# A gated cross-attention and low-rank feed-forward kernel: two small factors padded to 16 rows, the second first, the context's casts on GpSimd, and the first tile's low part multiplied last

## What is computed

```python
x = x + tanh(g_xattn[0]) * xattn(layernorm(x), ctx_1024)
x = x + tanh(g_ffn[0]) * ffn(layernorm(x), W, b, lora_down, lora_up, down_aux, up_aux)

def xattn(h, v):                       # softmax over the context's 77 rows
    p = softmax(einsum('bsd,bvd->bsv', h, v), axis=-1)
    return einsum('bsv,bvd->bsd', p, v)

def ffn(h, W, b, lora_down, lora_up, down_aux, up_aux):
    low = up_aux @ (lora_up @ (lora_down @ down_aux))
    return einsum('bsi,oi->bso', h, W) + b + einsum('bsi,oi->bso', h, low)
```

## Time and profile before

| | |
|---|---|
| median of 3 runs | 305.19 us (305.17 to 305.98) |
| the profiled execution, its whole time | 305.47 us |
| its span | 303.4 us |
| TensorE busy | 295.6 us |
| VectorE, GpSimd, ScalarE busy | 230.0, 224.5, 183.7 us |
| moved by DMA | 56.39 MB, mean 186 GB/s |

### The profile page before, as it was taken

One profiled execution on the slowest core, in us unless ns is written; L12 is line 12 of the kernel. 1 busy time (PEld: TensorE's weight loads), 2 busy tenths in 40 slices (PEclk: granted clock), 3 DMA queues, 4 the chain that ended last, 5 costly groups with the idle time before them and its releaser, 6 DMA issues.

```text
span 303.4 us, 6504 instructions
## 1 busy us (share of the span) xinstructions
PE 295.6 (97%) x2072; PEld 282.9 (93%) x2072; DVE 230.0 (76%) x797; ACT 183.7 (61%) x540; POOL 224.5 (74%) x274
## 2 busy tenths in 40 slices
PE   7999999999999999999999999999999999999992
PEld 5799999999999999999999999999999999999992
DVE  2877788885887788788498778777877788778865
ACT  2765675573775666566476666556665675567652
POOL 3478777785687877777578877787778777887763
PEclk9999999999999999999999999999999999999998
DMA  7754765442786494455265577544445555444003
GB/s 209 307 174 174 242 208 210 152 166 103 247 251 222 161 260 176 166 208 210 95 191 183 208 259 283 203 156 165 169 160 193 210 208 208 165 159 161 38 36 138
DMA packets 16750, 56.39 MB, mean 186 GB/s; under 512 B 2118, under 2 KB 2134, under 8 KB 16717
## 3 DMA queue, kind: packets, MB, share of 16 engines
q1 hardware_dynamic: 16281, 55.19, 52.7%
q10 hardware_dynamic: 436, 0.80, 0.8%
HBM read 35.84 MB, written 16.78 MB: 173 GB/s over the span
## 4 chain that ended last, share of the span: by engine, by line
PE 97%; DVE 1%; ACT 0%; issue 0%; POOL 0%; POOLq 0%; ACTq 0%; DVEq 0%
PE y_ps L598 68%; PE a_ps L647 10%; PE y_ps L652 10%; PE y_ps L629 2%; PE c_ps L588 2%; PE y_ps L565 1%; PE a_ps L605 1%; PE a_ps L570 1%; PE y_ps L697 0%; PE y_ps L616 0%; PE y_ps L705 0%; PE y_ps L701 0%; PE c_ps L579 0%; DVE o_sb L831 0%; ACT squares L498 0%
## 5 line engine op out<-in xcount | busy, mean ns | idle before, releaser
L598 PE MATMUL y_ps<-wc,xT 128*128 128x256 f32 x1524 | 224.9, 302 | 0.0
L598 PEld LDWEIGHTS y_ps<-wc,xT 128*128 128x128 f32 x1524 | 211.2, 189 | 2.0
L393 POOL TENSOR_TENSOR x_bias<-x,bias_g 128x512 f32<-128x512 f32 x63 | 81.5, 1294 | 58.2 <-DVE x L793 58.2
L381 POOL TENSOR_TENSOR xT<-xt_raw,xT 128x512 fp32r<-128x512 f32 x64 | 83.4, 1302 | 0.1
L484 ACT ACTIVATE expd<-y_ps,neg_max,rs 128x77 f32<-128x77 f32 x64 | 26.8, 418 | 81.1 <-DVE neg_max L780 81.1
L404 POOL TENSOR_TENSOR rs<-stat_eps,half_neg 128x2 f32<-128x2 f32 (+1 forms) x67 | 46.2, 689 | 5.2
L831 DVE SCALAR_TENSOR_TENSOR o_sb<-y_ps,rs,x_bias 128x512 f32<-128x512 f32 x64 | 47.5, 743 | 0.6 <-POOL rs L404 0.6
L498 ACT ACTIVATE squares<-x,x_nmean 128x512 f32<-128x512 f32 x64 | 45.4, 710 | 1.7 <-DVE x_nmean L801 1.6
L652 PEld LDWEIGHTS y_ps<-stacks,pT 110*128 110x128 f32 (+1 forms) x256 | 39.6, 190 | 5.7
L769 DVE BATCH_NORM_STATS2 bn<-x_sb 128x6 f32<-128x512 f32 x64 | 43.8, 684 | 0.0
L793 DVE SCALAR_TENSOR_TENSOR x<-a_ps,x_sb 128x512 f32<-128x512 f32 x64 | 43.4, 678 | 0.2 <-PE a_ps L647 0.2
(11 more groups left out here) (81 smaller groups left out, 192.6 us busy)
## 6 DMA issues: line engine op xcount, KB each, us to landing
x_sb<-in_x SPq DMA_DIRECT2D x32, 512.0 KB, 4.4
xt_raw<-in_xt SPq DMA_DIRECT2D x31, 512.0 KB, 5.2
out<-o_sb SPq DMA_DIRECT2D x31, 512.0 KB, 3.0
stacks<-v_hi SPq DMA_DIRECT2D x2, 308.0 KB
w_all<-in_w SPq DMA_DIRECT2D x2, 256.0 KB, 6.5
out<-o_sb SPq DMA_DIRECT2D x2, 256.0 KB, 2.0
stacks<-v_hi SPq DMA_DIRECT2D x2, 252.0 KB
stacks<-v_lo SPq DMA_DIRECT2D x2, 252.0 KB
```

The source lines that it names most:

```text
L381: pool.tensor_tensor(xT[:, k % TRING, 1, :, :], xt_raw[:, k % XRING // UNIT, k % UNIT, :, :], xT[:, k % TRING, 0, :, :].bitcast(F32), ALU. ...
L393: pool.tensor_tensor(x1_bias[:, q, :], x1[:, j, :], bias_g[:, :], ALU.add).then_inc(x1b_ready, 1)
L598: mm = pe.matmul(y_half(k, h)[:, 0:n], xT[:, k % TRING, part, c, :], wc[:, c, w, h * H:h * H + n], start=(c == 0 and part == 0 and w == 0) ...
```

## The change

- The host pads `low_in` from 100 to 112 rows and `low_out` from 50 to 64, with zeros (`whole_lanes`); more rows are loaded, but the padding of `low_in_sb` and `low_out_sb` adds only zeros to the products.
- On ScalarE's DMA queue low_out goes first, and the context's 77 rows follow as two DMAs, 64 and 13 rows; they stood first, as one.
- TensorE has five fillers instead of eight. The product for the second factor (up) comes first, and that of the first factor (down) after it in halves of 256 columns, the second half in another PSUM bank; ScalarE's and VectorE's copies are halved likewise (`down_hi`, `down_lo`), and the low-rank products wait for the half they need.
- VectorE finishes up_st ahead of centring the context.
- GpSimd, not ScalarE, makes v_hi of the first batch, and it, not ScalarE and VectorE, copies the columns `ct` into `wc`, around the cast of the first x.
- ScalarE takes the tanh of the gates before ct, not after it.
- VectorE makes v_lo ahead of W's low parts, not after them.
- In `first_scores` the products with W's high parts come first, then x's high part with the low parts, and x's low part last, with its own wait.

```diff
@@ -408,8 +412,16 @@
             def prep(n, k):
                 pass
+            pool.wait_ge(ld_ctx, 32)
+            pool.wait_ge(row0_ok, 1)
+            pool.wait_ge(tg_ok, 1)
+            pool.tensor_scalar(v_hi[0:VP, 0:D], c_rows[0:VP, :], tg[0:VP, 0:1], None, ALU.mult).then_inc(v_hi_ok, 1)
+            pool.wait_ge(ct_hi_ok, 1)
+            pool.tensor_copy(wc[:, :, 0, D:D + V], ct_part(0, 0)[:, :, 1:VP].bitcast(F32)).then_inc(c_cols, 1)
             xt_landed(pool, 0, 0)
             pool.tensor_copy(xT[:, 0, 0, :, :], xt_raw[:, 0, 0, :, :]).then_inc(x0_hi, 1)
+            pool.wait_ge(ct_lo_ok, 1)
+            pool.tensor_copy(wc[:, :, 1, D:D + V], ct_part(0, 1)[:, :, 1:VP].bitcast(F32)).then_inc(c_cols, 1)
             for k in (-2, -1):
                 step(k, k)
             pool.wait_ge(ld_b, 16)
@@ -418,19 +430,17 @@
         @block.scalar
         def _(act):
-            act.dma_start(c_rows[1:VP, :], ctx_in[0]).then_inc(ld_ctx, 16)
             act.dma_start(low_out_sb[:, :], low_out).then_inc(ld_out, 16)
+            cut = V // BY * BY
+            for a, z in ((0, cut), (cut, V)):
+                act.dma_start(c_rows[1 + a:1 + z, :], ctx_in[0, a:z, :]).then_inc(ld_ctx, 16)
             load_w(act, 1)
             act.dma_start(xt_raw[:, 0, 0, :, :].rearrange("p c r -> p (c r)"), xt_in[0, :, 0:D]).then_inc(ld_first_xt, 16)
             def ctx_rows_hi(n):
-                act.wait_ge(ld_ctx, 32 * n + 16)
-                if n == 0:
-                    act.wait_ge(row0_ok, 1)
-                    act.wait_ge(tg_ok, 1)
-                else:
-                    act.wait_ge(stacked[(n - 1) % 2], stack_landed(n - 1))
+                act.wait_ge(ld_ctx, 32 * n + 32)
+                act.wait_ge(stacked[(n - 1) % 2], stack_landed(n - 1))
                 if n == 2:
                     act.wait_ge(stacked[0], 16 * (FIRST + 3))
                 act.activation(v_hi[0:PACK[n], 0:D], c_rows[0:PACK[n], :], ACT.Copy, scale=tg[0:PACK[n], 0:1]).then_inc(v_hi_ok, 1)
@@ -537,22 +547,24 @@
                 if packs(t, TAKE):
                     ctx_product_hi(t // TB + 1)
+            def down_hi(h):
+                act.wait_ge(low_mm, 2 + h)
+                act.activation(dn_st[:, h * H:(h + 1) * H], down_bank(h), ACT.Copy).then_inc(dn_hi_ok, 1)
             act.wait_ge(low_mm, 1)
-            act.activation(dn_st[:, :], a_ps[0:LR, :], ACT.Copy).then_inc(dn_hi_ok, 1)
-            act.wait_ge(low_mm, 2)
             act.activation(up_st[:, :], up_bank(), ACT.Copy).then_inc(up_hi_ok, 1)
-            prep(0, TURN)
-            act.wait_ge(ct_hi_ok, 1)
-            act.activation(wc[:, :, 0, D:D + V], ct_part(0, 0)[:, :, 1:VP].bitcast(F32), ACT.Copy).then_inc(c_cols, 1)
+            down_hi(0)
+            down_hi(1)
             act.wait_ge(ld_w[0], 16)
             act.activation(tg[:, :], w_all[:, 0:2], ACT.Tanh).then_inc(tg_ok, 1)
             act.wait_ge(tg_ok, 1)
             act.activation(tg_row[:, :], tg[:, 0:1], ACT.Copy).then_inc(row_gate, 1)
+            prep(0, TURN)
             for c in range(KC):
                 act.wait_ge(w_tr, c + 1)
                 act.activation(wc[:, c, 0, 0:D], w_bank(c), ACT.Copy, scale=tg[:, 1:2]).then_inc(w_hi_ok, 1)
-            ctx_rows_hi(0)
             x_hi(1, 1)
             all_tiles(step, prep)
@@ -565,10 +577,19 @@
                     pe.matmul(y_ps[:, 0, 1, 0:P], ident[:, :], ident[:, :], start=True, stop=True)
             pe.wait_ge(ident_ok, 4)
-            stay_busy(8)
-            pe.wait_ge(ld_in, 16)
-            pe.matmul(a_ps[0:LR, :], low_in_sb[:, 0:LR], low_in_sb[:, LR:LR + D], start=True, stop=True)\
-                .then_inc(low_mm, 1)
+            stay_busy(5)
+            def low_up():
+                pe.wait_ge(ld_out, 16)
+                pe.matmul(up_bank(), low_out_sb[:, 0:LR], low_out_sb[:, LR:LR + D], start=True, stop=True).then_inc(low_mm, 1)
+            def low_down(h):
+                pe.wait_ge(ld_in, 16)
+                pe.matmul(down_bank(h), low_in_sb[:, 0:LR], low_in_sb[:, LR + h * H:LR + (h + 1) * H], start=True, stop=True)\
+                    .then_inc(low_mm, 1)
             def prep(n, k):
                 if k == TURN:
@@ -605,20 +626,27 @@
                 return pe.matmul(cw_ps(0), ct_part(0, lhs)[:, c, :], wc[:, c, rhs, 0:D], start=(c == 0 and lhs == 0 and rhs == 0),
                                  stop=(c == KC - 1 and rhs == 1), skip_group_check=True)
+            def score_part(c, part, w):
+                return pe.matmul(y_half(0, 1)[:, 0:H + VP], xT[:, 0, part, c, :], wc[:, c, w, H:H + H + VP],
+                                 start=(c == 0 and part == 0 and w == 0), stop=(c == KC - 1 and part == 1), skip_group_check=True)
             def first_scores():
-                pe.wait_ge(xl_ready, 1)
-                pe.wait_ge(c_cols, 2)
+                pe.wait_ge(x0_hi, 1)
+                pe.wait_ge(c_cols, 1)
                 pe.wait_ge(ct_lo_ok, 1)
                 for c in range(KC):
                     pe.wait_ge(w_hi_ok, c + 1)
-                    for part in range(2):
-                        pe.matmul(y_half(0, 1)[:, 0:H + VP], xT[:, 0, part, c, :], wc[:, c, 0, H:H + H + VP],
-                                  start=(c == 0 and part == 0), stop=False, skip_group_check=True)
-                        cw_part(c, part, 0)
+                    score_part(c, 0, 0)
+                    cw_part(c, 0, 0)
+                    cw_part(c, 1, 0)
+                pe.wait_ge(c_cols, 2)
+                for c in range(KC):
                     pe.wait_ge(w_lo_ok, c + 1)
-                    mm = pe.matmul(y_half(0, 1)[:, 0:H + VP], xT[:, 0, 0, c, :], wc[:, c, 1, H:H + H + VP],
-                                   start=False, stop=(c == KC - 1), skip_group_check=True)
+                    score_part(c, 0, 1)
+                pe.wait_ge(xl_ready, 1)
+                for c in range(KC):
+                    mm = score_part(c, 1, 0)
                 mm.then_inc(s_ready, 1)
                 for c in range(KC):
                     mm = cw_part(c, 0, 1)
@@ -701,16 +729,16 @@
                 pe.matmul(w_bank(c), dn_st[:, c * P:(c + 1) * P], up_st[:, :], start=False, stop=True,
                           skip_group_check=True).then_inc(w_tr, 1)
-            pe.wait_ge(ld_out, 16)
-            pe.matmul(up_bank(), low_out_sb[:, 0:LR], low_out_sb[:, LR:LR + D], start=True, stop=True)\
-                .then_inc(low_mm, 1)
+            low_up()
+            low_down(0)
+            low_down(1)
             prep(0, TURN)
             w_transposes(0)
-            pe.wait_ge(dn_ok, 1)
             pe.wait_ge(up_ok, 1)
-            low_rank(0)
-            for c in range(1, KC):
-                w_transposes(c)
+            for c in range(KC):
+                if c:
+                    w_transposes(c)
+                pe.wait_ge(dn_ok, 1 + c // 2)
                 low_rank(c)
             all_tiles(step, prep, T - 1)
             last_two()
@@ -869,22 +897,26 @@
                 if t == T:
                     output(t - 1, k - 1)
+            def down_lo(h):
+                dve.wait_ge(dn_hi_ok, 1 + h)
+                cols = slice(h * H, (h + 1) * H)
+                dve.tensor_tensor(dn_st[2 * LQ:LR, cols], down_bank(h)[2 * LQ:LR, :], dn_st[2 * LQ:LR, cols].bitcast(F32),
+                                  ALU.subtract).then_inc(dn_ok, 1)
             prep(0, STATS)
             dve.wait_ge(c_own, 1)
             ctx_mean(0)
-            prep(0, CENTRE)
-            dve.wait_ge(dn_hi_ok, 1)
-            dve.tensor_tensor(dn_st[2 * LQ:LR, :], a_ps[2 * LQ:LR, :], dn_st[2 * LQ:LR, :].bitcast(F32), ALU.subtract)\
-                .then_inc(dn_ok, 1)
             dve.wait_ge(up_hi_ok, 1)
             dve.tensor_tensor(up_st[LQ:2 * LQ, :], up_bank()[LQ:2 * LQ, :], up_st[LQ:2 * LQ, :].bitcast(F32),
                               ALU.subtract).then_inc(up_ok, 1)
+            prep(0, CENTRE)
+            down_lo(0)
+            down_lo(1)
             prep(0, TURN)
-            dve.tensor_tensor(wc[:, :, 1, D:D + V], ct_ps(0)[:, :, 1:VP], ct_part(0, 0)[:, :, 1:VP].bitcast(F32), ALU.subtract)\
-                .then_inc(c_cols, 1)
             dve.wait_ge(row_gate, 1)
             dve.memset(tg_row[0:1, :], 1.0).then_inc(row_gate_ok, 1)
+            ctx_rows_lo(0)
             for c in range(KC):
                 dve.wait_ge(w_hi_ok, c + 1)
@@ -910,6 +941,12 @@
             wide[:, 32 * q:32 * q + a.shape[1]] = a
         return wide
+    def whole_lanes(a):
+        rows = np.zeros((-(-a.shape[0] // 16) * 16, a.shape[1]), a.dtype)
+        rows[:a.shape[0]] = a
+        return rows
     b, n, d = x.shape
     xt = np.reshape(x, (b * n // (UNIT * 128), 128, UNIT, d // 128, 128))
     xt = np.reshape(np.transpose(xt, (0, 4, 2, 3, 1)), (b * n // (UNIT * 128), 128, UNIT * d))
@@ -921,8 +958,8 @@
     ins = {
         "x": x, "xt": xt, "ctx": ctx_1024, "w": np.concatenate([gates, rows], axis=1),
         "b": L0_ffn_b,
```

(4 more changed lines are left out.)

5 lines of the change are left out of this document (3 added, 2 removed).

## The result

The changed kernel takes 308.42 us, median of 4 runs (308.02 to 308.59); beside it the kernel before took 305.33 (4 runs): a ratio of 1.0089, 95% interval 1.0059 to 1.0118. The forecast was 304.6, in a range up to 305.6. It is slower by 3.1 us where 0.6 less was expected: rival 4, which had a chance of 0.08, came true, and with it rival 3.

What follows compares the result with a forecast made beforehand. TensorE bound it: 9.73 us of head, then one unbroken run of matmuls. The first low-rank product at 9.0 saves 0.7, taken as 0.6 off the median 305.19: 304.6 us, range 303.7 to 305.6.

Steps and rivals of the forecast that it cites:

- rival 4: TensorE's two pauses in the head: clock rises later, +2.3 us up to the scores less 0.7, 306.8 us; chance 0.08.
- rival 3: Context rows land last, at 7.1: first low-rank product at 10.1, 0.4 later than before, 305.6 us; chance 0.08.
- the prediction's own signs of being wrong: c_bn before 5.4 or after 6.7, v_hi far from 1.57, or W's four transposes at 0.9 instead of 0.44.
- low_out at 3.9: Head: second factor, first on ScalarE's queue, landed when the fillers end, so its product starts at 3.9; late bound 4.7.
- Context rows at 6.0: Second and third on ScalarE's queue: landing at 6.0, bounds 4.7 to 7.1, so c_cent ends at 8.2.
- First low-rank product at 9.0: After the transposes of c_cent and W: first L701 (L729 in the changed file) at 9.0 instead of 9.73.
- L619 at 16.1: Row behind the first scores (old L598) starts at 16.1 instead of 16.84, 0.7 earlier by the rounded terms.
- v_hi at 1.57: GpSimd's tensor_scalar for v_hi takes 1.57 us, like bias_g; 0.62, the casts' time, is the lower bound.
- rival 2: v_lo on VectorE meets GpSimd's cast: 0.3 us, or 0.62 for a full wait; 304.9 us; chance 0.12.
- Padding at nothing: Factors' loads: padded low_out would land nearer 3.5, hidden by the fillers; the sum has no cost for padding.
- insurance: First scores: x_lo's product last, past 14, hides x_lo's end at 12.9, which otherwise would cost about 1 us.
- Past 20 us: Behind the head everything hangs on the products' end: the same time line, shifted with it.

Runs made afterwards that it cites:

- the one with both pauses filled: Changed kernel with eight fillers ahead instead of five and seven more behind the down halves: 305.98 us, ratio 1.000.
- the run with the bridge: Kernel before with two fillers in its 0.6 us pause between W's first transposes and the first low-rank product: 305.13 us, ratio 0.9991.
- the run with eight fillers: Changed kernel with eight fillers at the start instead of five, nothing else: 309.41 us, ratio 1.0141.
- the old order: Changed kernel unpadded, context first in one transfer, down halves before up, v_lo last, eight fillers ahead, none behind the up product: 305.33 us, ratio 1.000.
- the run with v_lo last: Changed kernel with eight fillers ahead, seven behind the down halves, and v_lo behind W's low parts: 307.26 us, ratio 1.0044.
- GpSimd's part: Kernel before with v_hi and the copies of ct on GpSimd, v_lo early and the new order of first scores: 305.59 us, ratio 1.0015.
- no padding: Changed kernel with unpadded factors, eight fillers ahead and seven behind the down halves: 306.3 us, ratio 1.0037.
- the context on SyncE's queue: Changed kernel with eight fillers and the context's two DMAs issued by SyncE behind low_in, ahead of W: 307.02 us, ratio 1.006.

## Why the prediction was wrong, point by point

**The step that failed** is the clock's, which the sum left out and rival 4 carried: "both are short". Its place (the two pauses) and size were right: it forecast 2.3 us for the rounds at the lower level, and the profiles of the changed kernel and of the one with both pauses filled are 2.57 apart. Its chance was not. The argument for a small one was that today's pause of 0.6 at 9.1 costs nothing, which the run with the bridge bears out as far as can be told, but that pause comes with the clock already up. Here the first pause, 1.03, comes while it is still low, as in the kernel before with five fillers, where a pause of 0.81 there cost 2.1 us by itself; and the run with eight fillers shows a clock that was up fall to 0.50 in the second, 1.74 long there. Only filling both gave back the clock's whole part. Two of the prediction's own signs of being wrong came: the transposes at 0.85, and c_bn after 6.7. The Trainium skill, "TensorE: Matmul & The Clock Gate", Part 1, with low as the resting state and only sustained activity lifting it, was borne out by 0.85 for a group of transposes, and should have weighed more than one harmless pause.

**low_out at 3.9**: it landed about 5.0 (4.3 us after its issue at 0.72), and its product began at 5.11, beyond the late bound of 4.7, which made the first pause 1.03 us. That bound was the landing of another transfer, and it doesn't bind this one. The same transfer landed at 4.3 to 4.6 in the other runs with it padded and first, so it varies by 0.7; none landed by 3.9, and both profiles with five fillers ahead show a pause (1.03 and 0.45). The rule of the Trainium skill's "DMA: Bandwidth & Descriptors", section "Why a DMA increments its semaphore by 16 and not by 1", on rows and engines, was not borne out as a gain where it can be compared: in the old order low_in took 4.1 us from issue to landing with 112 rows and 4.13 with 100. For low_out in the new order no run shows the landing with 50 rows.

**Context rows at 6.0**: 7.07, at the late bound, rival 3. This is a second step that failed: with the clock restored the kernel takes 305.98, still above the range, by this landing and by c_cent beside v_hi (next point). The sum of kilobytes ahead of it was the wrong account: the bytes moved in time (1314 KB from 2.0 to 7.0, against 1319), yet the context was not among the first of them. Which transfers went ahead of it isn't shown. Its 1.1 us goes straight to c_bn, up_st and c_cent, which took 1.48 + 0.69 as worked out (7.10 to 9.30, forecast 2.17).

**First low-rank product at 9.0**: 10.63 on the time line, 0.90 later than before. With the clock restored it is 10.29, 0.56 later, the same 0.55 that L619 is later by. Of that, 0.3 is c_cent beside v_hi, which the prediction put at nothing and which the changed kernel, with its later v_hi, did not meet (c_cent 0.54). Without it the context rows cost some 0.25 here, and 0.14 in the run with v_lo last (9.87), where they landed at 6.93: rival 3's 0.4 was rather too much. In the changed kernel the lower clock adds 0.6: from the first transpose of c_cent to the product it is 1.29 (9.34 to 10.63), against 0.69 with the clock restored.

**L619 at 16.1**: 19.94. From the forecast: 1.3 for the late head (17.39, with the clock restored; 0.3 of it c_cent beside v_hi) and 2.55 for the clock.

**v_hi at 1.57**: 1.56. Taking the tensor_scalar's row over the casts' 0.62 was right. x0_hi and x_lo were hidden, as said.

**v_lo**: 1.39 instead of 0.74, that is 0.65 more, about the 0.61 of the cast beside it, and not the half that the sum of rival 2 took from the old clash. That was a misreading: v_lo had 0.42 left when x_lo began, and x_lo took 0.29 more. GpSimd's cast, begun while v_lo ran, shows the same rule in four runs: it lost 0.16, 0.29, 0.46 and 0.53 where v_lo had 0.29, 0.42, 0.58 and 0.66 left (eight fillers; both pauses filled; GpSimd's part; no padding), each time all but 0.13. Here the full wait of the Trainium skill's "SBUF — State Buffer", section "Who interferes with whom", agrees. It cost nothing in the changed kernel, since VectorE then waited for ScalarE; on the path of the kernel before it cost 0.45, and with the context on SyncE's queue v_lo was on the chain.

**Padding at nothing**: not contradicted for the changed kernel (both pauses filled, with it 305.98, without 306.3), wrong for the kernel before, where it costs 0.9. Putting x_lo's product last is what covers it, which is what I had called insurance.

**Past 20 us**: the same time line, shifted, as said: from L619 to the end of the span it is 286.6 us, as from L598 before. A row earlier than 16.84 need not keep this: the old order lost 0.34 behind it, the bridged kernel nothing.

## What to carry to other kernels

Where an unbroken run of matmuls follows a short head, the first question about the head isn't when each product starts but whether TensorE has anything to do in between: look for each new wait on TensorE ahead of the dense part, price it at the lower level for the whole stretch behind it, and give it a chance that fits. Cut fillers only after the transfer that they cover is seen to land early enough. And where two transfers share a queue and both are wanted first, exchanging them moves the wait; keep the products in the order in which their operands land.
